# First gates of batch 0 among the rounds of the matrix exponentials, and a new order of DVE's work on the experts' tiles

## The reference

```python
xn = layernorm(x) * w + b
g = xn @ gate_w + gate_b                      # 256 -> 512
gate, gate_gate = silu(g[..., :256]), silu(g[..., 256:])
u  = (xn * gate) @ state_w + state_b
Bm = gate_gate @ state_w + state_b
delta = softplus(mean(xn @ state_w + state_b, -1))
y  = scan(exp(-delta), delta * Bm * u)        # along the tokens
x  = x + y @ out_w + out_b                    # then a gelu MLP 256 -> 1024 -> 256
...
logits = xn2 @ moe_gate_w + moe_gate_b        # second block: top 2 of 8 experts
h  = gelu(xn2 @ ew1[e] + eb1[e]); eo = h @ ew2[e] + eb2[e]
moe = sum of the two chosen eo, weighted
for i in range(3): moe = moe @ expm(gens[i])  # three 256x256 exponentials
out = layernorm(x + residual + mix(abel_out, moe, sigmoid gate))
```

## Time and profile before

| | before |
|---|---|
| three runs | 750.4, 751.75, 752.8 us; median 751.75 |
| profiled execution | 751.1 us, of which the span from first to last instruction is 749.2 |
| busy, share of the span | TensorE 86%, DVE 79%, ACT 61%, POOL 33% |
| mean granted TensorE clock | 0.947 of full |
| experts' up products | 936 matmuls, 112.3 us busy, 13.2 us idle ahead of them |
| experts' down products | 936 matmuls, 110.4 us busy, 3.9 us idle ahead, 3.8 of it for DVE's `yb` |
| TensorE busy from 64.7 to 460.5 us | 379.3 of 395.8 us |
| silu table load on ACT at 40.88 | 1.28 us |

### The profile page before, as it was taken

The page is one execution under the profiler, slowest core; times in us unless marked ns, Lnnn a source line. Parts: engine busy times, 40 slices in busy tenths (PEclk is TensorE's granted clock), DMA queues, the critical chain, the costliest instruction groups (busy, mean ns, idle before and its releaser), DMA issues. The chain is left out here.

```text
span 749.2 us, 16171 instructions
## 1 busy us (share of the span) xinstructions
PE 640.8 (86%) x4525; PEld 470.1 (63%) x4526; DVE 593.1 (79%) x1543; ACT 455.9 (61%) x868; POOL 243.7 (33%) x295
## 2 busy tenths in 40 slices
PE   5789999999998999999989985799999999997000
PEld 4657557466574746657574864588888888886000
DVE  4878778899998989999798865577777777784593
ACT  3156483955648295564938342677777777784187
POOL 2003020214427062442606422034343433344042
PEclk9999999999999999999999999799999999999555
DMA  4643232164733536373845642466656555410873
GB/s 142 210 126 56 85 54 60 57 141 169 144 113 91 137 115 141 107 149 126 217 111 168 235 151 64 109 159 163 149 143 161 146 120 146 97 49 12 278 256 140
DMA packets 124502, 99.21 MB, mean 132 GB/s; under 512 B 60432, under 2 KB 114587, under 8 KB 124316
## 3 DMA queue, kind: packets, MB, share of 16 engines
q1 hardware_dynamic: 108028, 68.82, 32.1%
q0 software_dynamic: 16416, 29.67, 16.9%
HBM read 62.42 MB, written 33.68 MB: 128 GB/s over the span
## 5 line engine op out<-in xcount | busy, mean ns | idle before, releaser
L1831 POOL DMA_INDIRECT scratch_ys<-ye,place x78 | 82.9, 1063 | 155.1 <-ACT ye L1877 143.2
L58 PE MATMUL up<-xe_s,words 128*128 128x256 bf16 x936 | 112.3, 278 | 13.2 <-DVE xe_s L1981 13.2
L58 PE MATMUL bank<-words 128*128 128x512 bf16 (+1 forms) x576 | 109.2, 343 | 6.8 <-DVE logits L1022 4.1
L58 PE MATMUL down<-words,h_s_e 128*128 x936 | 110.4, 274 | 3.9 <-DVE yb L1965 3.8
L58 PEld LDWEIGHTS up<-xe_s,words 128*128 x936 | 93.3, 100 | 26.3 <-issue 13.9
L58 PEld LDWEIGHTS down<-words,h_s_e 128*128 128x128 bf16 x936 | 90.2, 98 | 19.1 <-issue 6.5
L58 PE MATMUL bank<-xn_s,mlp_w 128*128 128x512 bf16 x384 | 88.3, 383 | 2.5 <-DVE xn_s L747 2.5
L58 PEld LDWEIGHTS bank<-words 128*128 128x128 bf16 x576 | 55.1, 98 | 54.0 <-issue 7.6
L58 PE MATMUL bank<-mlp_w,shared 128*128 128x256 bf16 x768 | 86.4, 273 | 0.0
L476 POOL DMA_INDIRECT scratch_zs<-rows,pos x64 | 71.5, 1117 | 42.7 <-DVE pos L1072 24.0
L58 PEld LDWEIGHTS bank<-mlp_w,shared 128*128 128x128 bf16 x768 | 75.0, 98 | 10.6 <-issue 0.4
(11 more groups left out here) (243 smaller groups left out, 1152.3 us busy)
## 6 DMA issues: line engine op xcount, KB each, us to landing
xb<-scratch_zs SPq DMA_DIRECT2D x156, 64.0 KB
words<-scratch_ys SPq DMA_DIRECT2D x16, 514.0 KB, 8.7
scratch_abel<-staged SPq DMA_DIRECT2D x8, 514.0 KB, 5.0
abel_all<-scratch_abel SPq DMA_DIRECT2D x8, 514.0 KB
x_in<-in_x SPq DMA_DIRECT2D x8, 512.0 KB, 5.1
words<-in_out_b_row SPq DMA_DIRECT2D x8, 512.0 KB, 3.7
x_res<-in_mlp_b_row SPq DMA_DIRECT2D x8, 512.0 KB, 3.5
words<-in_x POOLq DMA_DIRECT2D x8, 512.0 KB, 7.8
```

The source lines that it names most:

```text
L58: last = nc.tensor.matmul(dst, lhs(a, k), rhs(b, k), start=start and n == 0, stop=stop and n == total - 1)
L1831: nc.gpsimd.indirect_dma_start(out=ys_dram[:, :], out_offset=bass.IndirectOffsetOnAxis(ap=place[:, k, s:s + 1], axis=0), in_=ye[:, k % 2, ...
```

## The change

Part 1, all of it in batch 0. On TensorE, `exponential_round` is cut into `round_turns` and `round_products`. `turn1(0)` moves between the turns and the products of round 1, `first_gates(0)` between rounds 1 and 2, `gates(0, 2..3)` between round 2 and the squaring loop, and `step_size(0)` behind the loop. For batch 0 the banks are others: gates use 6 and 7 twice (so that chunk 2 waits for silu 0 and chunk 3 for silu 1), the step size bank 7. On ACT `norm1(0)` moves ahead of round 2's copies, and the four silus and `gate_heads(0)` follow `out_w`'s heads ahead of the loop's copies. On DVE `norm1_split(0)` moves behind the tails of `gate_w`, ahead of round 1's combinations, and `gate_product(0)` and `gate_split(0)` follow the last combination of X ahead of the loop. One late product gets a wait for the magnitudes, whose bank it shares.

Part 2 and 3, in the experts' `body` on DVE. At tile 0, tile 1's tail and the split of tile 0's hidden values go ahead of the transpose of tile 2. In every fourth tile, `places` goes behind the bias sum.

```diff
+        def gate_bank(i, c):
+            return bank[6 + c % 2 if i == 0 else c]
+        def size_bank(i):
+            return bank[7 if i == 0 else 4]
...
# ACT
             for s in range(GENS):
                 turned_copy(s, s)
             weight_heads((0, 1))
-            for r in (1, 2):
-                for s in range(GENS):
-                    turned_copy(r * GENS + s, s)
-            weight_heads((2,))
+            for s in range(GENS):
+                turned_copy(GENS + s, s)
             act.wait_ge(vec_in, 16 * len(vectors))
             norm1(0)
+            for s in range(GENS):
+                turned_copy(2 * GENS + s, s)
+            weight_heads((2,))
+            silus(0, range(0, 2 * KC))
+            gate_heads(0)
...
# DVE
             weight_tails((0,))
+            norm1_split(0)
...
                 stt(X[:, s], mat(3 + s), scaled[:, 4:5], X[:, s]).then_inc(mat_r, 1)
-            norm1_split(0)
+            gate_product(0)
+            gate_split(0)
...
# TensorE
-            exponential_round(0, A, A)
-            exponential_round(GENS, A2, U, True)
-            exponential_round(2 * GENS, L, U, True)
+            round_turns(0, A)
+            round_products(0, A)
+            round_turns(GENS, A2)
             turn1(0)
+            round_products(GENS, U, True)
+            pe.wait_ge(w_tail, 1)
+            first_gates(0)
+            round_turns(2 * GENS, L)
+            round_products(2 * GENS, U, True)
+            gates(0, range(KC, 2 * KC))
             pe.wait_ge(sq_r, 6)
             squarings = pe.value_load(sq_i[0:1, 0:1], min_val=SQ_MIN, max_val=SQ_MAX)
             with pe.Fori(SQ_MIN - 1, squarings) as k:
-                exponential_round(k * GENS + (3 * GENS - LATE), X, X)
+                round_turns(k * GENS + (3 * GENS - LATE), X)
+                round_products(k * GENS + (3 * GENS - LATE), X)
+            pe.wait_ge(mean_done, 6)
+            step_size(0)
             pe.wait_ge(mat_r, squarings * GENS + (3 * GENS - LATE))
...
# experts, DVE, body(q, k)
                     turned(0, 0)
                     tails(0, 0)
                     turned(1, 1)
-                if not (isinstance(q, int) and q >= QT - 2):
-                    turned(q + 2, (k + 2) % RING)
-                if not (isinstance(q, int) and q == QT - 1):
-                    tails(q + 1, (k + 1) % RING)
-                split_hidden(q, k)
+                    tails(1, 1)
+                    split_hidden(0, 0)
+                    turned(2, 2)
+                else:
+                    if not (isinstance(q, int) and q >= QT - 2):
+                        turned(q + 2, (k + 2) % RING)
+                    if not (isinstance(q, int) and q == QT - 1):
+                        tails(q + 1, (k + 1) % RING)
+                    split_hidden(q, k)
+                    biased(q - 1, (k - 1) % RING)
                 if k % GROUP == 0:
                     places(q, k)
-                if not (isinstance(q, int) and q == 0):
-                    biased(q - 1, (k - 1) % RING)
```

More of the change, by code:

```diff
@@ L530, in late_copies, with silus, gate_heads @@
                     nc.scalar.activation(aT[:, n % GENS], mat(5), ACT.Copy).then_inc(late_copied, 1)
+            def silus(i, cs):
+                for c in cs:
+                    act.wait_ge(gate_done, 4 * i + c + 1)
+                    wait(act, g_tail if c < KC else gg_tail, i)
+                    dst = g if c < KC else gg
+                    nc.scalar.activation(dst[:, c % KC], gate_bank(i, c)[:, :], ACT.Silu,
+                                         bias=gate_b[:, c:c + 1]).then_inc(g_r, 1)
+            def gate_heads(i):
+                act.wait_ge(g_r, 4 * i + 4)
+                wait(act, b_done, 2 * i)
+                nc.scalar.activation(gg_s[:, 0], gg[:, :, :], ACT.Copy).then_inc(gg_head, 1)
             for s in range(GENS):
@@ L1581, in _ @@
                 j = i - LAG
[L1582 to L1584 removed]
                 if i > 0:
+                    first_gates(i)
                     turn2(i - 1)
[L1587 to L1590 removed]
+                    gates(i, range(KC, 2 * KC))
+                    step_size(i)
                 if i == 1:
```

72 lines of the change are left out of this document (32 added, 40 removed).

## The result

| | before | changed |
|---|---|---|
| median | 752.28 us (750.41 to 754.01) | 743.29 us (742.45 to 744.23) |
| ratio | | 0.9883, 95% interval 0.9858 to 0.9909 |
| profiled execution | 751.1, span 749.2 | 742.6, span 740.5 |

A forecast was written before the change was run, and what follows sets the result against it. TensorE was busy 86% of the span, so gains had to come where it stands still or works late. 3.0 + 1.3 + 3.9 + 0.9 = 9.1 off 751.1 gave 742.0 us; range 739.5 to 746.5, own range 739.5 to 744.5.

The forecast's parts named there:

- Part 1: Batch 0: gates among the exponential's rounds start states(0) at 50.7 against 53.70; 3.0 us gained, kept to the end.
- rival C's second half: Between 65 and 460 us the early work meets a bound that stands still: no measurable change; 0.07 with its first half.
- Rival A: Batch 0: the longer matrix chain eats Part 1's gain, states(0) starts at 53.7, total 745.0 us; chance 0.12.
- Rival D: Batch 0: TensorE's clock stays at 1.2 GHz through 24 us of full-speed work, 24 us more, 766 us; chance 0.03.
- Part 2: Experts' start: up(4) starts at 494.6 against 495.90, so 1.3 of 3.9 us is kept (ends 0.6 and 2.4).
- Part 3: Experts' loop: places behind the bias sum gains 3.9 of the 4.3 us excess (ends 2 and 4.3).
- Rival B: Experts' loop: places costs the same wherever it stands, Part 3 gives only its last 0.9, 745.9 us; chance 0.10.
- The end: Experts' end: from 677.03 to the last down takes 8.4 us against 9.35; 0.9 gained (0.3 to 1).

The follow-up runs named there:

- e10: Changed kernel with the next tile's gather ahead of the tags on SP and ACT's gate head copy behind the three turned copies: 737.13 us, ratio 0.9876.
- e3: Kernel before with only places moved behind the bias sum: 745.78 us, ratio 0.9972.
- e7: Kernel before with DVE reading the expert's number ahead of the split of the hidden values: 747.26 us, ratio 0.9931.
- e12: Kernel before with only the next tile's gather put ahead of the tags on SP: 746.22 us, ratio 0.9999.
- e5: Kernel before, unchanged, profiled again on another chip: 750.31 us, ratio 0.9995.
- e2: Kernel before with only tile 1's tail and tile 0's split ahead of tile 2's transpose: 746.27 us, ratio 0.9995.
- e6: Changed kernel, unchanged, run again on another chip: 743.52 us, ratio 0.9901 to the kernel before.
- e11: Changed kernel with POOL's first send held back until tile 5 has landed: 740.38 us, ratio 0.9919 to the kernel before.
- e8: Changed kernel with the next tile's gather issued ahead of the group's tags on SP: 740.60 us, ratio 0.9850 to the kernel before.
- e9: Changed kernel without Part 2 and with the next tile's gather ahead of the tags on SP: 740.32 us, ratio 0.9924 to the kernel before.
- e4: Changed kernel without Part 2, so Part 1 and Part 3 only: 740.77 us, ratio 0.9909 to the kernel before.
- e1: Kernel before with only Part 1, batch 0's gates among the rounds: 741.53 us, ratio 0.9919.

## Why the prediction was right, step by step

**Part 1, forecast 3.0, measured 4.4 to 5.0.** `states(0)` was forecast at 50.7 and starts at 49.56, the projection at 61.7 and starts at 60.32. The steps behind each other hold; the sizes do not quite. The squaring's turns start at 40.03, not 40.4, as groups of rows in one queue overlap by some 0.1 to 0.2 us (the second gates' row is 2.75 us long, the next starts 2.59 behind it). ACT's copies end the wait at 42.54, not 43.3: the 0.3 us for reading the loop's count is not there (gate_heads at 40.95, copies at 41.91), and again the rows overlap. The step size and the late turn take 1.73 us (47.83 to 49.56), not 2.1. Added up, 1.1 us. I added durations as the rows give them, where starts less starts would have shown the pitch.

The rest is the base. The start of batch 0 varies between executions: the projection starts at 64.71 to 66.38 in the six profiles without part 1 (mean 65.54) and at 59.63 to 61.29 in the seven with it but without e10's edit (mean 60.57). The difference of the means is 5.0, and the one profile of before that I worked from was the earliest of its six. Some 0.6 us of this has a name, and it is part 1's own:

```profile
40.66 6.95 PE L1519 MATMUL bank<-shared 128*128 128x256 f32 x24
```

```profile
40.66:47.61 6.95, 6.95 (x25) 5.54 (x24) 5.74 (x11) 1.94 (x3) 0.00 (x0) 0.77 0.42 133
```

These are the squaring's products in e3, and their window. Behind turns with the same 1.57 us of idle time as in the earlier trace rows the clock fell again: 0.77 was granted over the products, which took 6.95 us and not 5.34. It is so in three of the six profiles with the old order of batch 0 (6.95, 6.72 and 6.73 us in e3, e7 and e12), those in which round 1's products took over 8 us, and `states(0)` starts 16.6 us behind the squaring's turns there, not 15.45. In the eight profiles with part 1, where the gates stand in place of that wait, the products took 5.45 us each time, though round 1's took over 8 us in six of them. On average over the six that is 0.6 us which part 1 also takes away.

At the step size of batches 1 to 5 (93 to 267 us) the difference of the means stays at 4.96 to 4.97 us, so no bound stood still there, and rival C's second half is out. At the experts' first up product the means are 470.42 and 464.32, 6.1 us apart; the last 1.1 of it are within what profiles of the same kind differ by (468.95 to 472.22, and 462.58 to 465.38), and I do not count them as the change's. One such piece can be named: from the last count of the routing to `up(0)` the profile of before took 26.51 us and the changed kernel 25.48, but e5, the same program as before, took 25.42. In before, 16 matmuls of the fold there took 5.40 us at a granted clock of 0.52, in the changed kernel 3.72 us at 1.00.

**Rival A** asked for `states(0)` at 53.7 and a wait of 3 us ahead of the squaring's products. The wait is 1.04 us, "some 1 us" as forecast: ACT's row did get longer, and it took only that. e10 shows that even this could be had.

**Rival D, the clock.** The granted clock is 0.53 from 21.40 to 24.90 and 1.00 from 24.90 to 49.10, behind 4.05 us of idle time ahead of the products (4.92 in the earlier trace rows). The new order costs nothing there; by the rows of e3, e7 and e12 it spares a second fall.

**Part 2, forecast +1.3, measured -1.2 to -1.8.** From `up(0)` to down(4) are 34.40, 34.73 and 35.02 us in e2, e6 and the changed kernel, against 33.24 in before. This step failed. What it said of `up(1)`, `down(0)` and `up(2)` came true, and so did the place where the gain would be lost, tile 5's gather. The failing sentence is that SP "issues gathers and tags without a wait on DVE", from which I took the landing (29.7 us behind SP's first gather, or 0.7 later at most) as fixed. DVE got tile 5 at 30.8 (e6), 31.3 (e2) and 32.0. The landing is not fixed: SP loses 0.7 to 1.1 us on tile 3's gather beside the moved split, and the first results, and so POOL's sends, come 22.35 us behind SP's first gather and not 24.45 (479.69 and 488.01), where SP issues the tags. Where the sends are held back (e11: tile 5 at 29.9) `up(4)` does gain 0.9 us on `up(0)`, near the 1.3 forecast. The landing is not the whole loss either. Behind the wait for tile 5 I had put 0 of a possible 1.6 us for the clock: it was 0 in the changed kernel and in e2, and 1.6 in e6. And from `up(4)` to down(4) are 8.5 and 8.6 us in the former two, where the dense 7.9 of before had been taken for granted. I had asked of the moved work which engine comes next, and not which queue its results start and what runs beside it. And 0.0 to 0.9 us of a row that runs "beside two sends of POOL" had been used as a possible gain, when it was the price of being beside them. e8 and e9 show the forecast's sign right once the order on SP is mended: +1.0 to +2.5.

**Part 3, forecast 3.9, measured 4.15, or 0.2 to 0.7.** Where before runs in the slow rhythm, as in the profile that I had, the term is right (173.23 to 169.08), with its reasons: `yb` waits gone from the loop, pairs of 5.28. Where it runs in the quick one, the old order costs 0.2 to 0.7 us in all (169.26 to 169.75 against 169.07). e3 gained 2.1 us (1.0 to 3.2) there, more than these 0.7 and less than 4.8; what the rest is, its profile does not show. Rival B supposed that the catch-up of 0.4 us a tile leaves too little room behind the sum; what decides is the room ahead of it, and in the quick rhythm it is large enough for `places` on either side. The stall "once in four tiles" needs both the pause for the read of the expert's number (e7) and an idle time that the kernel before has in two of its comparisons and not in the other two, and one profile could not show the second.

**The end, forecast 0.9, measured 0.15.** The last down waits 1.09 us for the bias sum of the one before it, since no up product stands between them. I had put 0.45 us for that sum and nothing for the hand-over to DVE and back; from 673.73 to 677.65 are 3.92 us, of which 2.66 is the product and 1.26 the rest.

**The sum.** 4.4 + 1.8 - 1.8 + 4.15 + 0.15 = 8.7 us of span, against 3.0 + 0 + 1.3 + 3.9 + 0.9. Part 1 was 1.4 too small, part 2 3.1 too large, the end 0.75 too large, and 1.8 us between 65 and 470 us that the change is not shown to cause make up for most of it. The total is right partly by luck. Where the kernel before runs in the quick rhythm, the parts add up to some 4 us (5.0 - 1.5 + 0.5, an estimate). The changed kernel was not run there; the nearest, e4 and e11, are 6.8 and 6.0 us faster than before, as e1 is 6.1 us faster where part 1's 5.0 are shown, and this rest stays open. One bound was also added up wrongly: the named ends of the lower one (2.4, no pause, all of the 4.3, and 1 at the end) give 740.1 to 740.2, not 739.5.

## What to carry to other kernels

Before counting a gain from starting a stage earlier, follow its results too: which queue they start (here POOL's sends), and what runs at that time beside it (here SP's issues for the next tile), since a "fixed" landing is fixed only in the old company. Put the transfer that the next tile waits for ahead of the small ones that are wanted later: the edit is two lines in place of five, is worth nothing alone and 2.9 us together with the earlier start. And take a second profile before sizing a loop's stall: whether a periodic extra step costs anything was decided here by how far DVE had caught up when it came, and that made 4 us from one chip's runs to another's. The same goes for a short wait ahead of dense work: one profile showed the squaring at full clock behind 1.57 us of idle time, and three others of the same order did not.

## What the runs showed of the hardware

- The same loop has two rhythms, which go with the chip of the run and not with the kernel: an idle time of 0.3 to 0.5 us ahead of a late bias sum of DVE, 10 to 22 times in 32 tiles, in six profiles (the first pair and e5 to e8) and at most once in the eight others. Its cause stays open; e7 shows that it is not the read of the expert's number. Whether it is the chip or something in the run is not proven either, since each chip's runs came in one stretch.
- A read of one number from memory into a register costs DVE 0.74 to 0.80 us behind `places`, which has waits in it, and 0.05 to 0.09 us are left of it when it stands ahead of the split (e7: 1.66 us from `places` to the sum becomes 0.94).
- Single issues on SP's queue take far longer than the 0.5 us from one to the next within a tile. Beside POOL's sends in the changed kernel, 2.15 us lie between the third and the fourth tag (1.2 in e11 without sends) and 1.96 between the second and the third issue of tile 5's gather (0.52 in e11). But it happens without a send as well: in tile 3's gather in all six profiles with part 2, and once in the tags of e3 (1.74 us). And in e2 neither the tags nor tile 5's issues are stretched, yet the transpose starts 3.97 us behind the last issue (2.9 to 3.0 in e11 and in the changed kernel). So the sends are not shown to be the only cause, and the mechanism is open.
- How long the first products of the experts ran below full clock differed by the execution: `up(1)` took 4.11 us in e9, 4.37 in before and 5.30 in e4 after idle times of 3.3, 3.0 and 3.5 us. A difference of 1 us in this stretch between two profiles says nothing by itself, and the clock of both belongs beside it.
- A wait of 1.57 us ahead of 36 matmuls left the clock at 1.00 in three profiles (products of 5.34 to 5.35 us) and was followed by a lower one in three others of the same order (6.72 to 6.95 us).
